# Mixture of eight experts with two towers: GpSimd's adding DMAs for expert 1's first pair moved ahead of its clearing and of the gates' trip to DRAM

## What is computed

```python
h = jax.nn.relu(jnp.einsum('bi,eio->beo', x, eW1) + eb1)
h = jax.nn.relu(jnp.einsum('beh,eho->beo', h, eW2) + eb2)
expert_out = jnp.einsum('beh,eho->beo', h, eW3) + eb3
gates = jax.nn.softmax(jnp.einsum('bi,tie->bte', x, gW) + gb, axis=-1)
tin = jnp.einsum('bte,bed->btd', gates, expert_out)
th = jax.nn.relu(jnp.einsum('btd,tdh->bth', tin, tW1) + tb1)
th = jax.nn.relu(jnp.einsum('bth,tho->bto', th, tW2) + tb2)
out = jax.nn.sigmoid(jnp.einsum('bth,tho->bto', th, tW3) + tb3)
return out[..., 0]
```

## Time and profile before

| what | us |
|---|---|
| median of 3 runs | 578.03 (577.5 to 578.16) |
| the profiled execution's time | 578.84 |
| its span, first to last record | 577.0 |
| TensorE busy (PE) | 569.3, 99% of the span |
| VectorE busy (DVE) | 443.5, 77% |
| ScalarE busy (ACT) | 305.6, 53% |
| GpSimd busy (POOL) | 97.2, 17% |
| clock granted to TensorE | 9 tenths or more of full speed in all 40 slices |

### The profile page before, as it was taken

The page is one execution under the profiler, slowest core; times in us unless marked ns, Lnnn a source line. Parts: engine busy times, 40 slices in busy tenths (PEclk is TensorE's granted clock), DMA queues, the critical chain, the costliest instruction groups (busy, mean ns, idle before and its releaser), DMA issues.

```text
span 577.0 us, 8421 instructions
## 1 busy us (share of the span) xinstructions
PE 569.3 (99%) x2867; PEld 477.5 (83%) x2867; DVE 443.5 (77%) x555; ACT 305.6 (53%) x413; POOL 97.2 (17%) x102
## 2 busy tenths in 40 slices
PE   8999989999999999999999999999999999999998
PEld 5788868888888888888888888888888888888776
DVE  6955189976899759977799759978699767998493
ACT  3545085734665356633766347633757346654553
POOL 0000411033200521033110331024110332004000
PEclk9999999999999999999999999999999999999999
DMA  8532565466644676366644677366754676526100
GB/s 308 177 109 92 160 151 148 147 164 201 172 118 164 160 170 161 120 182 169 193 97 140 153 221 162 93 180 186 161 128 145 164 177 188 126 73 200 56 1 0
DMA packets 39406, 85.30 MB, mean 148 GB/s; under 512 B 3409, under 2 KB 8657, under 8 KB 39394
## 3 DMA queue, kind: packets, MB, share of 16 engines
q1 hardware_dynamic: 29970, 65.98, 34.4%
q0 software_dynamic: 9280, 18.91, 19.0%
q10 hardware_dynamic: 144, 0.26, 0.1%
HBM read 85.10 MB, written 0.04 MB: 148 GB/s over the span
## 4 chain that ended last, share of the span: by engine, by line
PE 90%; ACT 3%; DMA 2%; issue 2%; DVE 1%; POOL 1%; SPq 0%; ACTq 0%; DVEq 0%; POOLq 0%
PE psum L456 31%; PE psum L459 16%; PE psum L320 14%; PE psum L321 14%; PE psum L322 14%; DMA w_raw<-eW_first 1%; DMA w_raw<-eW_pairs 1%; ACT w_hi L698 0%; ACT h_hi L671 0%; DVE w_lo L909 0%; ACT h_hi L778 0%; ACT scratch L676 0%; PE psum L556 0%; POOL scratch L1267 0%; ACT scratch L779 0%
## 5 line engine op out<-in xcount | busy, mean ns | idle before, releaser
L909 DVE TENSOR_TENSOR w_lo<-w_raw,w_hi 128x1024 fp32r<-128x1024 f32 (+2 forms) x107 | 139.4, 1305 | 18.3 <-ACT w_hi L720 11.4
L320 PE MATMUL psum<-h_hi,w_hi 128*128 128x512 f32 (+1 forms) x340 | 131.8, 388 | 0.8 <-DVE h_lo L920 0.8
L321 PE MATMUL psum<-h_lo,w_hi 128*128 128x512 f32 (+1 forms) x340 | 131.6, 387 | 0.0
L322 PE MATMUL psum<-h_hi,w_lo 128*128 128x512 f32 (+1 forms) x340 | 131.4, 387 | 0.0
L456 PE MATMUL psum<-t_both,w_hi 128*128 128x512 f32 x448 | 122.2, 394 | 1.9 <-ACT scratch L727 1.9
L456 PE MATMUL psum<-x_both,w_hi 128*128 128x512 f32 x336 | 91.8, 394 | 0.4 <-DVE w_lo L909 0.2
L456 PEld LDWEIGHTS psum<-t_both,w_hi 128*128 128x128 f32 x448 | 77.0, 189 | 12.8 <-issue 2.1
L920 DVE SCALAR_TENSOR_TENSOR h_lo<-scratch,h_hi 128x512 fp32r<-128x512 f32 (+1 forms) x68 | 67.1, 989 | 26.4 <-ACT scratch L779 18.6
L459 PEld LDWEIGHTS psum<-t_both,w_lo 128*128 128x128 f32 x448 | 68.8, 189 | 9.5
L320 PEld LDWEIGHTS psum<-h_hi,w_hi 128*128 128x128 f32 x340 | 63.9, 188 | 14.0 <-DVE h_lo L920 1.2
L1280 POOL DMA_DIRECT2D w_raw<-eW_pairs x28 | 25.1, 897 | 297.5 <-DMA w_raw<-eW_pairs 297.1
(11 more groups left out here) (95 smaller groups left out, 625.7 us busy)
## 6 DMA issues: line engine op xcount, KB each, us to landing
w_raw<-eW_pairs SPq DMA_DIRECT2D x28, 768.0 KB, 4.2
w_raw<-eW SPq DMA_DIRECT2D x40, 512.0 KB, 3.9
scratch<-eW_pairs SPq DMA_DIRECT2D x28, 256.0 KB, 4.8
w_raw<-eW_pairs SPq DMA_DIRECT2D x28, 256.0 KB, 5.0
w_raw<-eW_pairs POOLq DMA_DIRECT2D x28, 256.0 KB, 5.0
scratch<-eW_pairs POOLq DMA_DIRECT2D x28, 256.0 KB, 6.5
scratch<-gates_dram POOLq DMA_DIRECT2D x8, 512.0 KB, 5.4
w_raw<-eW_first SPq DMA_DIRECT2D x7, 512.0 KB, 6.2
```

Source lines behind the costliest of these rows:

```text
L320: pe.matmul(bank, weights_hi, moving_hi, start=first, stop=False)
L321: pe.matmul(bank, weights_hi, moving_lo, start=False, stop=False)
L322: return pe.matmul(bank, weights_lo, moving_hi, start=False, stop=last)
L909: dve.tensor_tensor(wide(w_lo, slots), raw, wide(w_hi, slots).bitcast(F32), ALU.subtract).then_inc(slot_ready, 1)
```

## The change

`sum_blocks` is defined further up, and the call for expert 1's pair 0 with its two waits and two adding DMAs now stands ahead of all of steps 1 and 2 of GpSimd's order. Nothing else in the kernel is touched, and every DMA keeps its source, target and semaphore.

```diff
@@ -1260,12 +1260,22 @@
+            def sum_blocks(e, i):
+                count = 2 * (e - 1) + i // 2 + 1
+
+                pool.wait_ge(blocks_landed[i % 2], count * DMA)
+                pool.dma_start(raw_block(i, A21), blocks_dram(e, i, A22), accum_op=ALU.add) \
+                    .then_inc(s1_summed[i % 2], DMA)
+                pool.wait_ge(s3_landed[i % 2], count * DMA)
+                pool.dma_start(sums[:, S3[i % 2], :], blocks_dram(e, i, A21), accum_op=ALU.add) \
+                    .then_inc(s3_summed[i % 2], DMA)
+
+            sum_blocks(1, 0)
 
             pool.wait_ge(t_ready, NX)
             pool.wait_ge(h1_ready, K2)
             for n in range(T):
                 pool.memset(task_in[:, n * OUT3:(n + 1) * OUT3, :], 0.0).then_inc(added, 1)
-
             pool.wait_ge(gated_ready, 1)
             for t in range(T):
                 pool.dma_start(gates_dram[:, t, :], turned[t * E:(t + 1) * E, :]).then_inc(gates_stored, DMA)
@@ -1273,17 +1283,6 @@
             pool.dma_start(gates[:], gates_dram[0].partition_broadcast(P)).then_inc(gates_landed, DMA)
             pool.wait_ge(added, 2)
 
-            def sum_blocks(e, i):
...
-            sum_blocks(1, 0)
             for e in range(1, E):
                 for i in range(1, PAIRS):
                     sum_blocks(e, i)
```

## The result

The changed kernel takes **575.81 us** (median of 7 runs, 575.72 to 576.22); the kernel before takes 577.85 (577.15 to 578.49, 7 runs). The ratio is 0.9966, with a 95% interval from 0.9955 to 0.9978: 2.04 us faster, where 575.0 had been forecast and the range was 574.2 to 576.2. The profiled execution took 575.77, with a span of 574.0.

A forecast was written before the change was run, and what follows sets the result against it. TensorE, busy 569.3 of the 577.0 us span, bounds the kernel; closing its 3.03 us gap at expert 1 gives a span of 574.0, plus 1.03 makes 575.0 us, range 574.2 to 576.2 (8 in 10).

The forecast's parts named there:

- The gap and its place: TensorE's entry into expert 1, last matmul of layer 2 to P7: 3.03 us lost against expert 2, all to be closed.
- the range up to 0.37: Part of the 0.37 us lost ahead of P1 that might come from first entering the loop; taken as 0.
- rival A: Expert 1's first pass is partly slow for itself, so only part of the gap goes: 575.4 to 575.9 us; chance 0.13.
- The limit of 68.8 us for the landing: Pair 0's sums must land by 68.82 us for P3 to start without a gap; forecast landing 8.7 us ahead.
- the last line of the sum: Span 577.0 less 3.03 is 574.0; median 578.03 is span plus 1.03, giving 575.0 us.
- The durations of the DMAs: Pair 0's first adding DMA to take 6.02 us, landing at 60.1; the gates' fetch on GpSimd at 65.2 as before.
- VectorE beside GpSimd: Descriptors written only in VectorE's pauses would mean landing by 67.95 at worst, at no cost; not expected.
- the row at 82.70: A later adding DMA, issued at 82.70 with VectorE busy 1.97 of 2 us, landed in 5.0 us.
- Rival C: Gates' stores, now behind the adding DMAs, land late and delay pair 1; 580 us with 11 us of delay; chance 0.03.
- ScalarE's 77.46: Time when ScalarE wants pair 1's sums in expert 1; slowest landing forecast at 73.8, leaving 3.7 us of slack.
- Rival B: No change: pair 0's adding DMAs still land at 71 us or more; 578.0 us, or 577 at half the delay; chance 0.05.

The follow-up runs named there:

- behind the clearing: Against the changed kernel, both adding DMAs of expert 1's pair 0 put after GpSimd's clearing, still ahead of the gates' trip to DRAM; 575.82 us, ratio 0.9963.
- behind the stores: Against the changed kernel, both adding DMAs put after the clearing and the issue of the gates' two stores, ahead of the wait for their landing; 576.02 us.
- the last experiment: Against the kernel before, SP's loads of expert 1's pair 1 wait until the gates' stores have landed; 577.63 us, ratio 0.9997.
- the run with six clearings: Against the changed kernel, six extra clearings between the gates' fetch and pair 1's adding DMAs; 575.78 us, ratio 0.9969.
- the run with fourteen clearings: Against the changed kernel, fourteen extra clearings between the gates' fetch and pair 1's adding DMAs; 581.40 us, ratio 1.0069.
- the profiled run with nine clearings: Against the changed kernel, pair 0's adding DMAs put behind nine extra clearings, the gates' trip behind pair 1's sums; 580.49 us, ratio 1.0055.

## Why the prediction was right, and where it was not

**The gap and its place: right.** P1 at 74.85, P6 at 79.04, P3 at 80.44 and P7 at 81.84 stand within 0.02 us of the forecast. L698 at 61.45 was forecast to be 61.46, released by TensorE. Expert 2's P1 is at 141.35 (141.4). The entry into the loop costs nothing (0.23 us from start to start, where expert 2's takes 0.22), so taking 0 out of the range up to 0.37 was right, and rival A is out.

**The limit of 68.8 us for the landing: right**, and borne out by the nine profiles of the table: it is 5.82 us ahead of the last matmul of layer 2, against a measured lead of 5.80 for L698, which starts 0.1 behind a landing, so 5.90 for the landing. The 0.08 is P7's, which the working left out: 84.89 stands 13.11 us behind the old landing, so by the same steps its limit is 68.75, 5.89 ahead. Each microsecond behind it costs one.

**What failed is the last line of the sum**, "the median of the runs is 578.03, so span plus 1.03: 575.0". The time outside the span is a constant 1.8 us, and my own text had it ("span plus 1.8"). A median of 578.03 thus meant a span of 576.2, and the trace's 577.0 was a run with a long gap. The change takes away the gap, whatever its length, so the kernel after ends where the gapless span ends: 574.0 plus 1.8, 575.8. Measured: 575.81. I subtracted one run's gap from another run's time. Most runs of the kernel before lost about 1.8 us (a median span of 575.8 less 574.0), not 3.03.

That the measured time lies inside the stated range is in part luck. The range had been made wide enough for rival A, and 575.81 stands in A's band (575.4 to 575.9); but nothing of what A says is in the trace. By the time alone the wrong rival would have been believed.

**The durations of the DMAs: off, at no cost.** I took 6.02 and a fetch at 65.2; it was 4.1 and 62.03. The moved DMA meets a nearly empty stretch (the DMA engines' share is 0.11 from 55 to 56 us), and that shows the second thing that the place is worth. Beside SP's blocks, which go from 59.3 us on, the same DMA took 7.0 (behind the clearing), 7.7 (behind the stores) and 8.9 us (in the last experiment). Pair 1's blocks themselves, for which I had feared a later landing, land sooner: the 768 KB take 4.3 us and not 5.8.

**VectorE beside GpSimd: no loss**, as forecast from the row at 82.70. The two DMAs were issued with VectorE at work, 0.69 us at a time with pauses of 0.47, and landed in 4.1 and 4.6 us. Nor does VectorE explain the 7.0 us behind the clearing, at 58.58 with VectorE busy: behind the stores, at 59.97 with VectorE idle, it was 7.7. The lock that the Trainium skill describes in "SBUF — State Buffer", in the box on the "DVE blocks DMA" trap, is one for performance-mode instructions with two ports; here no delay of this kind shows.

**Rival C, slower: right in kind, wrong in its slack.** The stores' wait does grow behind adding DMAs, to 6.87 us in one experiment, though with the change itself, where the first of these had landed before the stores went, it was 2.44. But I gave pair 1's sums 2.35 us beyond ScalarE's 77.46, by looking at P1 of pair 1 alone. ScalarE's queue has `p5_take` of pair 0 behind L698 of pair 1, and so the slack is 0.8 us. What kept this rival away is the 3.7 us ahead of 77.46, which the run with six clearings bears out.

Rival B did not come true. That the loads of pair 2 would move forward with pair 0's splits did: 71.95 instead of 78.24.

## What to carry to other kernels

When a change removes a wait of varying length, forecast the time after it from the part that doesn't vary (here the gapless span plus the constant outside), and not by taking one trace's wait from the median. The profiled execution's own time, beside the median, says whether its wait was a long or a short one.

A deadline for a landing can be read from a later, undisturbed pass of the same loop, and it pays to look for it at every consumer in the queue, as the second one in line may bind first. And an early place in a queue is also a place among the transfers: the same DMA took 4.1 us in an empty stretch and 8.9 in a full one.

## What was unexpected of the hardware

**A long idle time of TensorE cost more than itself.** In the run with fourteen clearings TensorE had nothing to do for 3.46 us, up to 84.12. Stretches of this run (us, busy PE, PEld, DVE, ACT, POOL, clock granted to TensorE, DMA share, GB/s):

```profile
84.00:85.00 1.00, 0.88 (x4) 0.75 (x5) 1.00 (x1) 0.58 (x1) 0.00 (x0) 1.00 1.10 197
85.00:86.00 1.00, 1.00 (x6) 0.90 (x4) 0.78 (x2) 1.00 (x3) 0.00 (x0) 0.52 0.91 164
86.00:87.00 1.00, 1.00 (x4) 0.83 (x3) 1.00 (x2) 1.00 (x3) 0.00 (x0) 0.50 0.06 10
87.00:88.00 1.00, 1.00 (x4) 0.77 (x3) 0.34 (x1) 0.64 (x2) 0.00 (x0) 0.50 0.24 37
88.00:89.00 1.00, 1.00 (x7) 0.96 (x6) 0.17 (x1) 0.00 (x0) 0.00 (x0) 0.78 0.75 227
```

The granted clock fell from 1.00 to 0.50, from the upper to the lower of TensorE's two levels (2.4 and 1.2 GHz), about a microsecond after work had begun again, and came back within 88 to 89 us. P3 took 1.97 us and P7 2.54 instead of 1.40 each: 1.7 us on top of the wait of 3.6, which makes up the loss of 5.3. In the profiled run with nine clearings and in both profiles of the kernel before, whose longest idle time of TensorE there was 1.9 us, the clock stayed at 1.00. So a slower outcome would have been priced too low by one microsecond for one.

**An adding DMA of 256 KB took anything from 4.0 to 9.5 us**, over all profiles; the first one of expert 1's pair 0 from 4.1 to 8.9. The two stores of 16 KB made GpSimd wait 1.54 us with nothing beside them, 6.87 us behind two adding DMAs issued just before and with 1.3 MB of loads beside, and 5.43, 3.98 and 2.44 us with the same loads beside (the kernel before in two profiles, and the changed kernel). Why these three differ, and so what it is in the move that shortens the wait, no run here shows.
